# A GRU with its z gate last, experts with renumbered rows, and no matmul of a zero tile

## The reference

```
def cell(h, x):                      # scan over the 512 tokens, 4 sequences at once
    gi = x @ W_ih + b_ih; gh = h @ W_hh + b_hh
    i_r, i_z, i_n = split(gi, 3); h_r, h_z, h_n = split(gh, 3)
    r = sigmoid(i_r + h_r); z = sigmoid(i_z + h_z)
    n = tanh(i_n + r * h_n)
    return (1 - z) * n + z * h
hs = scan(cell, cond, x)             # initial state: cond
x = x + diff_attention(hs)           # two causal softmaxes, their difference filtered along time,
                                     # RMS norm, @ Wout
y = full_attention(adaptive_rms_norm(x, cond))   # o + o @ W_out
x = x + moe(y)                       # 64 experts, the best 6 of each token, capacity 128:
                                     # hid = silu(g) * u; eo = (hid @ down) * w; plus a shared expert
```

## Time and profile before

| | us |
|---|---|
| three timed runs, median (lowest, highest) | 5335.4 (5332.8, 5342.6) |
| the profiled execution | 5339.9 |
| its span, first to last instruction | 5338.3 |
| gate inputs, 0 to the barrier | 218 |
| GRU: loading `W_hh`, then 512 steps to 2510.8 | 18 + 2275 |
| diff attention | about 900 |
| filter, full attention | about 260, 694 |
| routing, experts, combination | about 320, 460, 190 |
| mean granted clock of PE over the span | 0.932 |

### The profile page before, as it was taken

One profiled execution on the slowest core, in us unless ns is written; L12 is line 12 of the kernel. 1 busy time (PEld: TensorE's weight loads), 2 busy tenths in 40 slices (PEclk: granted clock), 3 DMA queues, 4 the chain that ended last, 5 costly groups with the idle time before them and its releaser, 6 DMA issues. The chain is left out here.

```text
span 5338.3 us, 122278 instructions
## 1 busy us (share of the span) xinstructions
PE 4216.6 (79%) x49614; PEld 2121.2 (40%) x50173; DVE 2219.7 (42%) x5558; ACT 1013.3 (19%) x2550; POOL 284.0 (5%) x306
## 2 busy tenths in 40 slices
PE   7788888888888888887999999677787879577840
PEld 3344444444444444443444444333333334244420
DVE  1244444444444444444555555333544443211124
ACT  1111111111111111111232333122333321011100
POOL 0000000000000000000000000000000003300025
PEclk9899999999999999999999999788999989788975
DMA  1310000000000000000101010101111111167756
GB/s 56 112 61 0 0 0 0 0 0 0 0 0 0 0 0 0 0 0 20 42 28 41 28 41 28 66 16 49 42 41 41 41 49 56 52 212 224 243 171 160
DMA packets 172112, 255.94 MB, mean 48 GB/s; under 512 B 27094, under 2 KB 110294, under 8 KB 170034
## 3 DMA queue, kind: packets, MB, share of 16 engines
q1 hardware_dynamic: 140690, 184.66, 10.9%
q0 software_dynamic: 25440, 70.08, 4.4%
q10 hardware_dynamic: 5952, 0.81, 0.1%
HBM read 147.43 MB, written 62.92 MB: 39 GB/s over the span
## 5 line engine op out<-in xcount | busy, mean ns | idle before, releaser
L254 PE MATMUL gru_prz<-gru_whh,h 128*8 128x256 f32 x16384 | 982.1, 380 | 286.4 <-DVE h L332 286.4
L254 PEld LDWEIGHTS gru_prz<-gru_whh,h 128*8 128x8 f32 x16384 | 402.9, 90 | 756.2 <-DVE h L332 433.9
L315 DVE STREAM_TRANSPOSE gru_trz<-gru_prz 128x256 f32<-128x256 f32 x512 | 230.6, 450 | 883.7 <-PE gru_prz L254 883.7
L254 PE MATMUL gru_pn<-gru_whh,h 128*8 128x128 f32 x16384 | 542.3, 273 | 0.0
L254 PEld LDWEIGHTS gru_pn<-gru_whh,h 128*8 128x8 f32 x16384 | 449.7, 90 | 107.7 <-issue 0.5
L289 ACT ACTIVATE gru_rz<-gru_pre 128x32 f32<-128x32 f32 x512 | 118.7, 232 | 1509.0 <-DVE gru_pre L317 1509.0
L267 PE MATMUL gru_pw<-gru_warm 128*128 128x512 bf16 x1022 | 304.0, 379 | 81.0 <-issue 81.0
L324 DVE TENSOR_TENSOR_SCAN gru_narg<-gru_tn,gru_rz 128x128 f32<-128x128 f32 x512 | 217.4, 425 | 67.5
L246 PE MATMUL gru_pn<-gru_bias,gru_one 128*8 128x128 f32 x4096 | 207.7, 275 | 20.6 <-DVE h L310 20.6
L1326 PE MATMUL ex_pg<-ex_wg,ex_xT 128*128 128x384 f32 x512 | 218.6, 580 | 0.0
L461 ACT ACTIVATE da_probT<-da_ps 128x1024 f32<-128x1024 f32 (+3 forms) x256 | 180.2, 704 | 195.2 <-PE da_ps L432 194.0
(11 more groups left out here) (256 smaller groups left out, 5010.4 us busy)
## 6 DMA issues: line engine op xcount, KB each, us to landing
ex_wg<-in_L_ffn_gate_up_proj SPq DMA_DIRECT2D x64, 768.0 KB, 5.8
ex_wd<-in_L_ffn_down_proj SPq DMA_DIRECT2D x64, 384.0 KB, 7.0
xg<-gru_zeros POOLq DMA_DIRECT2D x4, 4096.0 KB, 35.5
da_hb<-wide SPq DMA_DIRECT2D x16, 1024.0 KB, 4.7
fa_hb<-xnT SPq DMA_DIRECT2D x16, 1024.0 KB, 4.5
ex_xg<-xg SPq DMA_DIRECT2D x64, 256.0 KB, 2.8
eo<-ex_eo POOLq DMA_DIRECT2D x64, 256.0 KB, 6.7
da_wg<-ahead SPq DMA_DIRECT2D x48, 256.0 KB, 4.8
```

What stands on the lines that cost most here:

```text
L254: last = nc.tensor.matmul(rows[32 * j:32 * j + 2 * B, 0:(g1 - g0) * P].rearrange("p (g f) -> p g f", f=P), t.h[:, c * B:(c + 1) * B, 1:4:2 ...
L315: nc.vector.transpose(trz[:].rearrange("p c x -> p (c x)"), prz[:, 0:2 * P]).then_inc(trz_done, 1)
```

## The change

1. *Gate inputs.* All 64 transposes of x run first, into `xT`, which now takes the large tile `wide` (free until the GRU writes its states there). x has two buffers, loaded ahead; the biases are loaded last. Only r and n go to `giT` (32 values for each token). The z inputs are computed the other way round, tokens as output rows: 16 blocks of 32 tokens for each of the four sequences, in four column groups, 256 matmuls of 512 columns, and DVE adds the bias into `giz`.
2. *GRU.* Three gates of 16 matmuls and 128 columns each: r, n, z. The input of z comes by four matmuls that pick the token's row out of `gru_zin` with columns of the identity (`add_z_input`), ahead of the step, and POOL copies the next 32 tokens' rows to `gru_zin` once in 32 steps; so PE's loop has 32 steps in its body. z has its own transpose and sigmoid. The new state is written as (h - n) * z + n: a subtraction on DVE in place of 1 - z and z * h, and the last scan uses z and n.
3. *Zero tiles.* `gru_pw` and every `keep_warm` are gone, with their tiles.
4. *Experts.* The 512 rows of an expert's `gate_up_proj` go to partition p as rows 4p to 4p+3 (before: p, 128+p, 256+p, 384+p), those of `down_proj` as rows 2q and 2q+1. The transposes take every fourth feature and every second hidden column, so that the sums stay the same.

```
         @block.tensor
         def _(pe):
             pe.wait_ge(ident_in, 16)
-            with pe.Fori(0, B) as b:
-                pe.wait_ge(x_in, b * 16 + 16)
+            for b in range(B):
+                pe.wait_ge(x_in[b % 2], 16 * (b // 2 + 1))
                 for k in range(KD):
...
+            with pe.Fori(0, B) as b:
+                gates(b)
+            for kb in range(T // 32):
+                if kb >= 4:
+                    pe.wait_ge(z_out, kb - 3)
+                for k in range(KD):
+                    for b in range(B):
+                        last = nc.tensor.matmul(pg[32 * b:32 * b + 32, kb % 4, :], xT[:, b, k, 32 * kb:32 * kb + 32], wih[:, k, D:2 * D],
+                                                start=(k == 0), stop=(k == KD - 1))
+                last.then_inc(z_psum, 1)
...
+            with pool.Fori(1, T // 32) as kb:
+                pool.wait_ge(zin_used, kb * 1)
+                nc.gpsimd.tensor_copy(zin[:], t.giz[:, bass.ds(kb, 1), :].rearrange("p o f -> p (o f)")).then_inc(zin_ready, 1)
...
+            def add_z_input(kb, tl):
+                if tl == 0:
+                    pe.wait_ge(zin_ready, kb * 1 + 1)
+                pick = t.ident[:].rearrange("p (b t) -> p b t", b=B)[:, :, tl]
+                for j in range(KD):
+                    last = nc.tensor.matmul(pz[32 * j:32 * j + B, 0:P], pick, zin[:, j * P:(j + 1) * P], start=True, stop=False)
...
+            def gate(rows, g, start, done):
+                for c in range(KD):
+                    of = t.h[:, c * B:(c + 1) * B, 1:4:2].rearrange("p b o -> p (b o)") if g != 1 else t.h[:, c * B:(c + 1) * B, 3]
+                    for j in range(KD):
+                        last = nc.tensor.matmul(rows[32 * j:32 * j + (B if g == 1 else 2 * B), 0:P], of, whh[:, c, g, j, :],
+                                                start=(c == 0 and start), stop=(c == KD - 1))
+                last.then_inc(done, 1)
+
             def step(s):
...
                 pe.wait_ge(h_ready, s * 1 + 1)
-                for rows, g0, g1, done in ((prz, 0, 2, rz_rows), (pn, 2, 3, n_rows)):
...
+                gate(pr, 0, True, r_rows)
+                gate(pn, 2, False, n_rows)
+                gate(pz, 1, False, z_rows)
+
+            def between(s, kb, tl):
+                pe.wait_ge(tn_done, s * 1 + 1)
+                add_bias()
+                pe.wait_ge(tz_done, s * 1 + 1)
+                add_z_input(kb, tl)
...
-                for _ in range(WARM):
-                    nc.tensor.matmul(pw[:, :], warm[:, 0:P], warm[:, :], start=True, stop=True)
...
+            with pe.Fori(0, T // 32 - 1) as kb:
+                for tl in range(32):
+                    step(kb * 32 + tl)
+                    between(kb * 32 + tl, kb + (tl + 1) // 32, (tl + 1) % 32)
...
+                nc.scalar.activation(cb(d1[:, :, 3]), narg[:, :, 1:2 * B:2], ACT.Tanh).then_inc(tanh_done, 1)
+                act.wait_ge(tz_done, s * 1 + 1)
+                nc.scalar.activation(cb(d0[:, :, 3]), tz[:, :, 0:B], ACT.Sigmoid).then_inc(z_act, 1)
...
-                z = rz[:, 1, :, 0:2 * B:2]
-                nc.vector.tensor_scalar(cb(d0[:, :, 3]), z, -1.0, 1.0, ALU.mult, ALU.add).then_inc(side, 1)
-                nc.vector.tensor_tensor(cb(d1[:, :, 3]), z, cb(state), ALU.mult).then_inc(side, 1)
-
-                dve.wait_ge(side, s * 2 + 6)
+                dve.wait_ge(z_rows, s * 1 + 1)
+                nc.vector.transpose(tz[:].rearrange("p c x -> p (c x)"), pz[:, 0:P]).then_inc(tz_done, 1)
                 dve.wait_ge(tanh_done, s * 1 + 1)
+                nc.vector.tensor_tensor(cb(d1[:, :, 2]), cb(state), cb(d1[:, :, 3]), ALU.subtract).then_inc(less_n, 1)
+
+                dve.wait_ge(less_n, s * 1 + 1)
+                dve.wait_ge(z_act, s * 1 + 1)
...
-        self.keep_warm(0, 3)
...
-        self.keep_warm(4, 5)
...
-                core.keep_warm(5, 4)
...
-            sp.dma_start(wg[:, u, :, :], gate_up[bass.ds(e, 1), :, :].rearrange("o (k p) i -> p (o k) i", p=P)).then_inc(w_in[u], 16)
-            sp.dma_start(wd[:, u, :, :], down[bass.ds(e, 1), :, :].rearrange("o (c q) h -> q (o c) h", q=HC)).then_inc(w_in[u], 16)
+            sp.dma_start(wg[:, u, :, :], gate_up[bass.ds(e, 1), :, :].rearrange("o (p k) i -> p (o k) i", p=P)).then_inc(w_in[u], 16)
+            sp.dma_start(wd[:, u, :, :], down[bass.ds(e, 1), :, :].rearrange("o (q c) h -> q (o c) h", q=HC)).then_inc(w_in[u], 16)
...
-                    last = nc.tensor.transpose(px[:, u % 2, k * P:(k + 1) * P], xg[:, v, k * P:(k + 1) * P], t.ident[:])
+                    last = nc.tensor.transpose(px[:, u % 2, k * P:(k + 1) * P], xg[:, v, k:D:KD], t.ident[:])
...
-                    last = nc.tensor.transpose(ph[0:HC, s % 2, c * P:(c + 1) * P], hid[:, s % 2, c * HC:(c + 1) * HC], t.ident[:])
+                    last = nc.tensor.transpose(ph[0:HC, s % 2, c * P:(c + 1) * P], hid[:, s % 2, c:I:2], t.ident[:])
```

More of the change, by code:

```diff
@@ L76, in _ @@
             sp.dma_start(t.ident[:], t.const["ident"]).then_inc(ident_in, 16)
[L77 to L81, removed]
+            for b in range(B):
+                if b >= 2:
+                    sp.wait_ge(xT_psum, (b - 1) * KD)
+                sp.dma_start(xin[:, b % 2, :, :], x[b, :, :].rearrange("(tt p) d -> p tt d", p=P)).then_inc(x_in[b % 2], 16)
+            for n, bvec in enumerate((b_ih, b_hh)):
+                sp.dma_start(zbias[:, n, :], bvec[D:2 * D].unsqueeze(0).broadcast_to([P, D])).then_inc(zb_in, 16)
         @block.gpsimd
@@ L101, in _, with gates @@
                     last.then_inc(xT_psum, 1)
-                pe.wait_ge(w_spread, 3 * KD)
-                pe.wait_ge(xT_ready, b * KD + KD)
-                for c in range(GC):
+            pe.wait_ge(w_spread, 3 * KD)
+            pe.wait_ge(xT_ready, B * KD)
+            def gates(b):
+                for c in range(NG):
                     if c >= 4:
-                        pe.wait_ge(gi_even if c % 2 == 0 else gi_odd, b * (GC // 2) + (c - 4) // 2 + 1)
+                        pe.wait_ge(gi_even if c % 2 == 0 else gi_odd, b * (NG // 2) + (c - 4) // 2 + 1)
+                    col = GATES[c // KD] * D + (c % KD) * P
@@ new lines, in _ @@
+            for k in range(KD):
+                copy_x(k)
+            for k in range(KD):
+                spread_w(k)
+                for n in range(3):
+                    copy_x(KD + 3 * k + n)
+            dve.wait_ge(b_in, 16 * (4 * KD))
+            nc.vector.tensor_tensor(bias[:, 0, 0:KD], bias[:, 0, 0:KD], bias[:, 1, 0:KD], ALU.add).then_inc(bias_ready, 1)
+            dve.wait_ge(zb_in, 32)
+            nc.vector.tensor_tensor(zbias[:, 0, :], zbias[:, 0, :], zbias[:, 1, :], ALU.add).then_inc(zbias_ready, 1)
@@ L248, in step @@
             def step(s):
                 pe.wait_ge(h_ready, s * 1 + 1)
-                for rows, g0, g1, done in ((prz, 0, 2, rz_rows), (pn, 2, 3, n_rows)):
-                    for c in range(KD):
-                        for j in range(KD):
-                            last = nc.tensor.matmul(rows[32 * j:32 * j + 2 * B, 0:(g1 - g0) * P].rearrange("p (g f) -> p g f", f=P),
-                                                    t.h[:, c * B:(c + 1) * B, 1:4:2].rearrange("p b o -> p (b o)"),
-                                                    whh[:, c, g0:g1, j, :],
-                                                    start=(c == 0 and g0 == 0), stop=(c == KD - 1))
-                    last.then_inc(done, 1)
+                gate(pr, 0, True, r_rows)
@@ L271, in _ @@
+            with pe.Fori(0, T // 32 - 1) as kb:
+                for tl in range(32):
+                    step(kb * 32 + tl)
+                    between(kb * 32 + tl, kb + (tl + 1) // 32, (tl + 1) % 32)
+            for tl in range(31):
+                step(T - 32 + tl)
+                between(T - 32 + tl, T // 32 - 1, tl + 1)
             step(T - 1)
@@ L375, in setup @@
         dve.wait_ge(self.core_set, self.SET)
-    def keep_warm(self, bank, n):
-        for _ in range(n):
-            self.nc.tensor.matmul(self.ps[:, bank, :], self.warm[:, 0:P], self.warm[:], start=True, stop=True)
     def tensor(self, pe, it, v, q, ident, identb, mask, maskT):
```

133 lines of the change are left out of this document (72 added, 61 removed).

## The result

The changed kernel is slower: 5,424.6 us, median of four timed runs (5,416.0 to 5,434.2), against 5,334.1 for the kernel before on the same chip; ratio 1.0173, with an interval of 1.0145 to 1.0201. The forecast was 5,080, and 0.93 on faster. The profiled execution has a span of 5,425.4 us, 87.1 more than before.

| stage | before, us | after, us | difference | forecast |
|---|---|---|---|---|
| gate inputs | 217.9 | 212.0 | -5.9 | -10 |
| GRU, with its load | 2294.2 | 2103.2 | -191.0 | -276 + 30 |
| diff attention | 899.5 | 1197.5 | +298.0 | -20 + 24 |
| filter | 247.0 | 247.5 | +0.5 | 0 |
| full attention | 709.1 | 732.8 | +23.7 | -14 + 24 |

What follows compares the result with a forecast made beforehand. The GRU step's serial chain across engines, 512 steps and 2,273 us of 5,338.3, was taken as the bound. Terms -10 - 276 + 30 + 15 - 15 = -256 gave 5,080 us (median), range 4,980 to 5,180 with late z.

Steps and rivals of the forecast that it cites:

- Zero matmuls in the attentions: Taking them out of both attentions: -20 - 14 + 48 for lower clock, net +15 us, bounds -34 and +75.
- the gain is paid back: Rival: full fetch waits at PE's jumps and both attentions at the lower clock, 5,190 us; chance 0.10.
- a clock under 0.85 in either attention: Sign of being wrong: the clock of diff or full attention, 0.98 and 0.91 before, drops under 0.85.
- a jump over 4 us: Sign of being wrong: PE's jump back in the GRU loop, taken as 2.1 us, costs over 4 us.
- The GRU step: Recurrence with separate gates: step from 4.44 to 3.90 us, 512 times, -276 us, bounds -328 and -225.
- The jump: PE's 14 jumps back in the 32-step GRU loop: a fetch of 2.1 us each, +30 us, bounds 0 and +45.
- Gate inputs: Stage ahead of the GRU, transposes of all sequences moved ahead: -16 + 7.4 - 1, -10 us, bounds -15 and -3.
- The joins: Gate inputs: at each of four joins PE still waits 1.9 us for the last eviction, so 7.4 us come back.
- Experts: Expert stage with renumbered rows: shorter loads -35, strided transposes +20, net -15 us, bounds -70 and +30.
- the strided reads: Experts' transposes reading every fourth float: +20 us, half of the 38 if their loading doubled.
- the longer runs of the loads: Experts' weight loads in longer runs shorten PE's waits: 1.1 us in each of 32 pairs, -35 us.
- The doubling: Experts: if the loading in the strided transposes doubled, they would add some 0.6 x 64 = 38 us.

Runs made afterwards that it cites:

- e1: The changed kernel with all three groups of zero matmuls put back in both attentions; 5,094.1 us, ratio 0.9571.
- e3: The changed kernel with only the five zero matmuls behind the transposes of the maxima put back in both attentions; 5,146.4 us.
- e7: The kernel before without the three zero matmuls of each GRU step, those of the attentions kept; 5,374.6 us beside 5,367.9 before.
- e9: e1 with no loop on PE, all 512 GRU steps written out; 5,069.1 us, ratio 0.9459 to the kernel before.
- e12: e9 with the three zero matmuls in both attentions, five in full attention only, four nowhere, and 16 fills of 1 MB; 5,042.7 us, ratio 0.9390.
- e10: The kernel before with only the experts' rows renumbered (longer load runs, strided transposes); 5,340.3 us, ratio 0.9961.
- e11: The kernel before with only the experts' transposes strided, loads as they were, so products of mismatched rows; 5,376.2 us, ratio 1.0004.

## Why the prediction was wrong

**The term that failed** is "Zero matmuls in the attentions": +15 us, bounds -34 and +75, against +322 by the two stages (+330 between the changed kernel and e1). It failed at one sentence: "I take 3 us a round more of it", that is of the lower clock. It was 44 us a round in diff attention. I had seen that PE does little for some 2.8 us once the zero matmuls are gone, and that each us at the lower clock in the PE-bound part costs half of itself. The second is about right: 44.4 or 47.8 us cost 19. The first did happen, but e3 shows that the idle part of it, 1.34 us, does not lose the clock by itself. What I took for granted was that a fall lasts about as long as its cause, as the dips of the kernel before seem to. In its diff attention there are three behind the first projections: one of 10.2 us that ends just behind the three zero matmuls, one of 6.8 us that ends in them, and one of 3.4 us (3204.1 to 3207.5) that ends among the scores. Timeline of the kernel before, PE, in the round with the second dip and then, in two lines, the end of the third, which I could have read for this:

```profile
2825.61 0.60 PE L399 MATMUL da_ps<-da_maskb,da_identb 128*128 128x128 bf16 x4
...
2827.82 0.97 PE L380 MATMUL da_ps<-da_warm 128*128 128x512 bf16 x2 [0.22 <-issue]
2828.85 1.09 PE L408 MATMUL da_ps<-ident,da_spread 128*128 128x128 f32 x8
2829.78 1.24 PE L380 MATMUL da_ps<-da_warm 128*128 128x512 bf16 x5
2830.95 1.13 PE L425 MATMUL da_ps<-da_rot,da_kp 32*128 32x512 f32 x4
...
3206.73 0.61 PE L399 MATMUL da_ps<-da_maskb,da_identb 128*128 128x128 bf16 x4
...
3207.77 0.40 PE L399 MATMUL da_ps<-da_maskb,da_identb 128*128 128x128 bf16 x4
```

The mask products (L399) run at half speed up to the zero matmuls, the transposes of the maxima behind these at full speed (1.09 us, and 1.24 for the five). In the diff attention of before the clock is never down from L425 to the sums, so no row shows how long it would stay so. The bound on the other side was the whole rest of a round at 1.2 GHz, from L425 to the next projections: 22 us of PE's work taking 44 in its place, 16 times, less what the waits cover. It came out as 19 a round. My bounds held the cost of the fall at twice a guess and not at what the rows allowed (and twice the guess gives -20 - 14 + 96 = +62, where I wrote +75). The rival "the gain is paid back" took the same +75 as its price, so the case that came was in no rival either. It did stand among the signs that I would be wrong: a clock under 0.85 in either attention, and a jump over 4 us.

**The GRU step** was right: 3.90 forecast, 3.905 measured, and 511 such differences are 272 us. No step was late by z or by the new waits, and the clock did not fall within a block; e7 shows that the old step did not need its zero matmuls either.

**The jump** was under-sized: 2.1 us each, bounds 0 and 3.2, against 4.76. (By the rule that I gave, up to two loads of 1.7 us less 0.5, the upper bound was 2.9.) The wait is 3.1 us, at the end of my range; the other 1.6 us, the clock that falls in it, I left out. The forecast that a jump is a fetch was right (496 packets for 450), and e9 shows it. The first steps' 14.6 us were in no term: I weighed the fills for GpSimd's queue and not for PE's fetch, beside a DMA share of 0.85; e12 shows most of them gone with smaller fills.

**Gate inputs**: -5.9 for -10. The sum has a wrong sign: a start 1 us later costs 1 us, so -16 + 7.4 + 1 is -8. The joins took 1.9 us, z's block 55.1 us, as worked out; but the gates' first record is at 32.96 us and not at 28 to 31, and PE waits 14.6 us in all for x to arrive. **Experts**: -21 by the timed runs of e10 for -15; the strided reads cost 2 us (-12 to +17 by e11's interval) for my 20, and the longer runs of the loads, e11 less e10, brought 23 (some 19 to either side) for 35. The doubling that would cost the full 38 did not come: the loads grew by half.

With the attentions' term at its real size and the jump at 4.76, the sum is -6 - 272 + 67 + 15 + 322 - 21 = +105 us; the medians differ by 90 and the profiles by 87, where the experts had 38 for 21.

## What to carry to other kernels

Before a filler matmul is taken out, look at what PE runs behind it up to the next place where the clock is seen to come back, and price that whole stretch at the lower clock, not the gap alone: here a round lost 19 us, not 1.5. Test each group by itself; here the cheapest one (3 matmuls in a wait) did all of the work in one stage, two were needed in another, and none in a third. A loop on PE whose body must be fetched again pays some 5 us for each jump: closed every 8 steps it lost all of the gain, written out whole it gained 60 us more. Keep bulk DMA out of the time in which PE streams new instructions.

## What the runs showed of the hardware

- In diff attention PE was busy for 44.4 of 44.4 us with 32-row products, products of 32 output rows and masks, and the granted clock stayed at 1.2 GHz all the time, to come back near the end of the sums; in the GRU, products with 8 and 4 output rows ran on at 2.4 GHz, in e7 with PE busy for only 72% of the time. I had expected a busy PE to come back. That 32-row products in general hold it down does not follow: among the scores, also of 32 rows, it came back after 3.4 us (before and e3).
- A taken jump of PE's to a body of 1,792 records or more: 4.8 to 6.2 us, of which 3.1 to 4.1 are a wait for the fetch and the rest mostly the lower clock behind it; two instruction packets more for each. A body of 224 records: no fetch, but 0.19 us a step for the end of a pass (4.096 against 3.905).
- Written out in sequence (e9), PE's instructions come at one packet of 16 KB in 4.3 us and always in time, except beside the 16 MB of fills at the start, where one step took 8.52 us for 3.9.
